# Two 64-row blocks to a tile, 75 chunks of edges for 78, and a load queue in the order of the stages

## What is computed

```python
# x [2048, 256], adj [2048, 2048], 8 heads of 32
scores = einsum('hnd,hmd->hnm', x * 32 ** -0.5, x2)
attn = softmax(where(adj > 0, scores, NEG))
x = layernorm(x + einsum('hnm,hmd->hnd', attn, v))
...
h = (x @ W_w.T + W_b)                       # second layer
e = leaky_relu(s_src[:, None] + s_dst[None, :], 0.2)
attn = softmax(where(adj == 0, NEG, e), axis=1)
out = layernorm(x + elu(attn @ h))
```

## Time and profile before

| | us |
|---|---|
| Median of 3 runs | 427.37 |
| The runs | 425.29, 427.37, 427.52 |
| The profiled execution's own time | 423.61 |
| Its span | 422.0 |
| VectorE busy | 298.7 (71%) |
| TensorE busy | 246.4 (58%) |
| GpSimd busy | 216.9 (51%) |
| ScalarE busy | 166.2 (39%) |

### The profile page before, as it was taken

The page is one execution under the profiler, slowest core; times in us unless marked ns, Lnnn a source line. Parts: engine busy times, 40 slices in busy tenths (PEclk is TensorE's granted clock), DMA queues, the critical chain, the costliest instruction groups (busy, mean ns, idle before and its releaser), DMA issues.

```text
span 422.0 us, 5435 instructions
## 1 busy us (share of the span) xinstructions
PE 246.4 (58%) x1394; PEld 175.0 (41%) x1394; DVE 298.7 (71%) x833; ACT 166.2 (39%) x473; POOL 216.9 (51%) x327
## 2 busy tenths in 40 slices
PE   0583454924677679778697988212571281396690
PEld 0463331613355457556464655111360160274460
DVE  2998498999999998999797858702350352657873
ACT  5414365432372464664425253000100251445635
POOL 7238556461775877726766311772777176164100
PEclk9995585795569686969798996655877575586886
DMA  8929618742776674412532400341444154142201
GB/s 294 375 52 372 262 68 283 237 117 99 259 251 211 209 306 122 121 39 66 147 121 57 123 29 29 92 112 35 112 112 108 38 131 106 55 115 77 67 25 56
DMA packets 24515, 57.93 MB, mean 137 GB/s; under 512 B 6592, under 2 KB 14912, under 8 KB 22432
## 3 DMA queue, kind: packets, MB, share of 16 engines
q0 software_dynamic: 10032, 31.77, 26.9%
q1 hardware_dynamic: 14448, 25.77, 17.1%
HBM read 53.20 MB, written 4.33 MB: 136 GB/s over the span
## 4 chain that ended last, share of the span: by engine, by line
PE 15%; DVE 14%; another core or an unknown queue 11%; issue 8%; POOL 6%; ACT 3%; DMA 1%; DVEq 0%; ACTq 0%; POOLq 0%
PE e_po L1445 8%; POOL e_ring L1071 5%; DVE e_weighted L1719 2%; PE e_pj L1468 2%; DVE e_y L1491 1%; DVE e_raw L1521 1%; DVE e_run L1690 1%; DVE e_run L1692 1%; DMA out<-e_prod 1%; DVE e_rden L1489 1%; DVE e_left L1719 1%; PE e_po L1426 1%; PE e_pq L1391 1%; DVE e_y L1742 1%
## 5 line engine op out<-in xcount | busy, mean ns | idle before, releaser
L1071 POOL DMA_INDIRECT e_ring<-in_kv,e_col_i x78 | 79.7, 1022 | 70.0 <-DVE e_col_i L1623 27.0
L1071 POOL DMA_INDIRECT e_ring<-table,e_col_i x78 | 74.4, 954 | 55.5 <-issue 23.0
L1445 PE MATMUL e_po<-e_weighted,e_sel_edges 128*128 128x264 f32 x158 | 52.0, 474 | 9.2 <-DVE e_weighted L1719 6.2
L1426 PE MATMUL e_po<-e_mean_row,e_diagonal 128*128 128x264 f32 x64 | 24.8, 479 | 37.5 <-DVE e_y L1491 22.9
L1445 PEld LDWEIGHTS e_po<-e_weighted,e_sel_edges 128*128 128x128 f32 x158 | 34.3, 232 | 19.5 <-DVE e_weighted L1719 9.8
L1164 ACT ACTIVATE e_search<-e_search 128x2048 bf16<-128x2048 int32 x16 | 30.5, 1908 | 26.4 <-DVE e_raw L1521 12.1
L1521 DVE MAX8 e_raw<-e_search 128x8 bf16<-128x512 bf16 (+2 forms) x56 | 38.7, 724 | 0.8
L1489 DVE RECIPROCAL e_rden<-e_po 128x8 f32<-128x8 f32 x32 | 6.5, 203 | 44.4 <-remote 20.2
L1391 PE MATMUL e_pq<-e_left,e_sel_rows 128*128 128x256 bf16 x156 | 33.3, 312 | 0.0
L1426 PEld LDWEIGHTS e_po<-e_mean_row,e_diagonal 128*128 128x128 f32 x64 | 12.6, 226 | 42.0 <-issue 40.5
L1445 PE MATMUL e_po<-e_left,e_search 128*128 128x264 f32 x84 | 27.9, 494 | 1.7 <-DVE e_left L1719 1.7
(11 more groups left out here) (221 smaller groups left out, 602.9 us busy)
## 6 DMA issues: line engine op xcount, KB each, us to landing
e_search<-in_adj SPq DMA_DIRECT2D x16, 1024.0 KB
table<-e_hx SPq DMA_DIRECT2D x16, 136.0 KB
e_ring<-in_kv SPq DMA_DIRECT2D x1, 2112.0 KB, 13.2
out<-e_prod SPq DMA_DIRECT2D x16, 128.0 KB
e_ring<-in_kv,e_col_i POOLq DMA_INDIRECT x78
e_ring<-table,e_col_i POOLq DMA_INDIRECT x78
e_xres<-in_x SPq DMA_DIRECT2D x2, 512.0 KB
e_xres<-in_x SPq DMA_DIRECT2D x3, 256.0 KB, 10.7
```

Of the source, the lines that this page charges most:

```text
L1071: nc.gpsimd.indirect_dma_start(out=rings[layer][:, q % RING[layer], :], out_offset=None, in_=kv if layer == 0 else table, in_offset=bass.I ...
L1426: nc.tensor.matmul(po[n % 2][:, 0:CV], diagonal[:, n % 3, :], mean_row[:], start=True, stop=False)
L1445: last = nc.tensor.matmul(po[n % 2][:, 0:CV], selection(layer, q, 1)[:, 0, :], weighted[plan.weighed_into(b)][:, j * CV:(j + 1) * CV], sta ...
```

## The change

- **Tiles.** A tile is no longer 128 consecutive rows but two blocks of 64 (`TILES`), one dense and one less dense from the fourth tile on. Every load of `adj` and x, every store to `table` and to the output becomes two transfers of 64 rows; the second halves of the first two tiles go out on ScalarE's queue.
- **Tables.** `CHUNKS` adds up to 75 (the big tile 13 instead of 16), `SEGS`, `GROUPS` and `KEEP` follow. The groups hold 7, 13, 12, 14, 15, 8 and 6 chunks instead of 8, 16, 12, 16, 9, 11 and 6, so the points at which GpSimd waits in layer 1 become q = 17, 30, 42, 56 and 71.
- **SyncE.** The w block goes out where the list puts the stage `w`, which now needs the load of the fifth tile; x of a later group goes out behind the loads of its own tiles.
- **Planner.** `FORESIGHT` goes from 0.1 to 0.2, and `w` is priced at 9.5 us on SyncE and 4 us more.

```diff
+BLOCK = 64
+TILES = ((0, 12), (1, 6), (2, 5), (3, 30), (4, 13), (7, 8), (9, 14), (10, 11), (15, 27), (16, 26), (17, 23), (18, 24), (19, 22), (20, 31), (21, 25), (28, 29))
-CHUNKS = (16, 8, 6, 5, 5, 4, 4, 4, 4, 4, 3, 3, 3, 3, 3, 3)
-SEGS = (16,) + (8,) * 2 + (4,) * 7 + (2,) * 6
+CHUNKS = (13, 8, 7, 5, 5, 5, 4, 4, 3, 3, 3, 3, 3, 3, 3, 3)
+SEGS = (16, 16, 8, 8) + (4,) * 8 + (2, 2, 4, 2)
-GROUPS = ((1,), (0,), (10, 11, 12, 13), (6, 7, 8, 9), (4, 5), (2, 3), (14, 15))
-KEEP = (24, 0, 16, 16, 24, 24, 16)
+GROUPS = ((2,), (0,), (8, 9, 10, 11), (6, 7, 12, 13), (3, 4, 5), (1,), (14, 15))
+KEEP = (24, 0, 16, 16, 24, 32, 16)
-FORESIGHT = 0.1
+FORESIGHT = 0.2
-    put("SP", 0.0, 0.0, ("w",), lag=34.0)
+    put("SP", 9.5, 0.5, ("w",), ("load", 4), lag=4.0)
-        put("SP", 0.0, 0.0, ("x", g), lag=(10.0, 12.0)[g] if g < 2 else 35.0)
+        put("SP", 1.2 * len(GROUPS[g]) if g > 1 else 0.0, g - 1.0 if g > 1 else 0.0, ("x", g), ("load", max(plan.k0[g] + len(GROUPS[g]) - 1, 5)) if g > 1 else None, lag=5.0 if g > 1 else (10.0, 12.0)[g])
...
-                sp.dma_start(adj_tile[:, k % 2, :], adj[t * P:(t + 1) * P, :]).then_inc(adj_loaded[k % 2], 16)
+                for i in range(1 if k < 2 else 2):
+                    sp.dma_start(adj_tile[half_of(i), k % 2, :], adj[rows_of(t, i), :]).then_inc(adj_loaded[k % 2], 16)
...
+                for j, t in enumerate(GROUPS[g]):
+                    for i in range(2):
+                        sp.dma_start(xres[half_of(i), plan.k0[g] + j, :], x[rows_of(t, i), :]).then_inc(x_loaded[g], 16)
...
             load_adj(2)
             load_adj(3)
-            sp.wait_ge(s("cleared"), 4)
-            sp.dma_start(w_sb[:], w_nat.rearrange("(k p) c -> p k c", p=P)).then_inc(s("w_loaded"), 16)
...
-            for g in range(2, NG):
-                load_x(g)
             for stage in stages:
                 if stage[0] == "load" and stage[1] >= 4:
                     load_adj(stage[1])
+                elif stage[0] == "w":
+                    sp.wait_ge(s("cleared"), 4)
+                    sp.dma_start(w_sb[:], w_nat.rearrange("(k p) c -> p k c", p=P)).then_inc(s("w_loaded"), 16)
...
+                elif stage[0] == "x" and stage[1] >= 2:
+                    load_x(stage[1])
...
+            for k in range(2):
+                act.dma_start(adj_tile[half_of(1), k, :], adj[rows_of(plan.order[k], 1), :]).then_inc(adj_loaded[k], 16)
             nc.scalar.preload_act_table_set("natural_log_exp_and_others")
```

More of the change, by code:

```diff
@@ L272, in listed @@
         g = plan.group_of_q(q)
-        return ("find_big", (q - plan.q0[g]) // 4 * 4 + 3) if g == BIG_GROUP else ("find", g)
+        return ("find_big", min((q - plan.q0[g]) // 4 * 4 + 3, plan.C[g] - 1)) if g == BIG_GROUP else ("find", g)
     def turned(layer, q):
@@ L296, in list_stages @@
             for p in range(parts_of[k]):
-                time = (3.35 if big else 0.8 if parts_of[k] == 4 else 1.3) + (1.25 if p == 0 else 0.0) + (2.5 if big else (0.9 if KEEP[g] == 16 else 1.35) if p == parts_of[k] - 1 else 0.0)
+                time = (3.35 if big else 0.8 if parts_of[k] == 4 else 1.3) + (1.25 if p == 0 else 0.0) + (2.5 if big else (0.45 * (KEEP[g] // TOP)) if p == parts_of[k] - 1 else 0.0)
                 kept_free = g and not big and p == parts_of[k] - 1
@@ L1010, in _ @@
                     sp.wait_ge(s("row_ready"), k + 1)
-                    sp.dma_start(table[t * P:(t + 1) * P, :], hx[:, k % 2, :]).then_inc(table_stored[k % 2], 16)
+                    for i in range(2):
+                        sp.dma_start(table[rows_of(t, i), :], hx[half_of(i), k % 2, :]).then_inc(table_stored[k % 2], 16)
                 elif stage[0] == "out":
@@ L1017, in _ @@
                     sp.wait_ge(s("emitted"), k + 1)
-                    sp.dma_start(out[t * P:(t + 1) * P, :], y_out[:, k % 2, :]).then_inc(out_stored[k % 2], 16)
+                    for i in range(2):
+                        sp.dma_start(out[rows_of(t, i), :], y_out[half_of(i), k % 2, :]).then_inc(out_stored[k % 2], 16)
         @block.gpsimd
@@ L1039, in _ @@
                 nc.gpsimd.memset(tile_base[:, k:k + 1], float(P * plan.c_first[t])).then_inc(s("const_ready"), 1)
-            nc.gpsimd.indirect_dma_start(out=xres[:, 0, :], out_offset=None, in_=x, in_offset=bass.IndirectOffsetOnAxis(ap=first_rows[:], axis=0)).then_inc(x_loaded[0], 16)
+            for i in range(2):
+                pool.dma_start(xres[half_of(i), 0, :], x[rows_of(plan.order[0], i), :]).then_inc(x_loaded[0], 16)
             pool.wait_ge(s("const_ready"), 3)
```

62 lines of the change are left out of this document (31 added, 31 removed).

## The result

| | before | with the change |
|---|---|---|
| Median, us | 427.12 (4 runs) | 442.32 (4 runs, 441.18 to 443.14) |
| Ratio to before, 95% interval | | 1.0415 (1.0373 to 1.0457) |
| Profiled execution, us | 423.61 | 442.53 |
| Its span, us | 422.0 | 440.9 |
| VectorE busy, us | 298.7 | 298.8 |

The change makes the kernel 4.2% slower. The forecast was 423.8 with a range up to 431.0: it had the sign wrong and the time lies outside the range.

A forecast was written before the change was run, and what follows sets the result against it. VectorE was taken to bound layer 0, gathers to pace layer 1. Start -1.5, VectorE's work -1.4, end of layer 0 -0.6, layer 1 -0.5, output +0.4 gave -3.6 us: 427.37 to 423.8, range 416.5 to 431.0.

The forecast's parts named there:

- The start: Up to the big tile's first round: VectorE idles 4.9 us instead of 6.9; -1.5 us, from -6 to +4.7.
- it is issued at about 20.0 instead of 32.99: On SyncE's queue at the start: the fifth tile's load leaves before the w block, once the third tile's sign is done.
- The rule against the change: Loads of adj into 64 partitions at half rate: third tile's sign 2.6 us later, time 426.4; chance 0.10.
- the block's length: SyncE's w block at the start: taken as 12.4 us, between bounds of 12.2 and 19.15.
- VectorE's work: Layer 0: draws +1.6, keep +1.1, fewer rounds -1.7, fewer chunks -0.8 for each of three lines; sum -1.4 us.
- In this stretch it counts in full: Layer 0: the -1.4 us of VectorE's work shortens the kernel by the whole amount.
- End of layer 0: Last tiles normed and projected: half of a projection half saved, -1.0, one more store issue, +0.4; -0.6 us (0 to -4).
- Layer 1: Gathers -3.75, first pause +1.3, tail +2.0: -0.5 us (-4 to +8); last output in two issues +0.4.
- The gathers set the pace: Layer 1: gathers of 0.94 us with 0.30 between, 1.25 us each, set its pace, interrupted by pauses.
- the tail of 29 chunks: Layer 1 from q = 71 on: 29 chunks to finish instead of 26, +2.0 us (0 to 3.8).
- The w block comes late: Rival at the start: block keeps 19.15 us, prefix sum at 45.0, VectorE waits; start +4.7, time 430.0; chance 0.12.
- the slow halves: Rival on loads of adj: halves at half rate, start +1.1, time 426.4; chance 0.10.

The follow-up runs named there:

- e10: The change, unedited, run again on a later chip beside the kernel before: 398.27 us, ratio 1.024 to the kernel before.
- e1: The kernel before with each adj load cut into two transfers of 64 neighbouring partitions, nothing else: 438.86 us, ratio 1.028 to the kernel before.
- e3: The changed kernel with halves interleaved in even and odd partitions instead of 0 to 63 and 64 to 127: 435.95 us, ratio 1.021 to the kernel before.
- e11: The same kernel as e3, on the chip of e10: 389.24 us, ratio 1.000 to the kernel before.
- e2: The kernel before with its own tiles, tables and whole-tile loads, and only SyncE's new order: 424.18 us, ratio 0.993 to the kernel before.
- e9: The kernel before, unedited, on the chip of e10: 389.61 us, ratio 0.999.
- e13: The change with sum_w behind the prefix sum, later turn_src behind the first turn, and stacked adj tiles in one transfer each: 622.71 us, ratio 1.470.
- e14: The change, unedited, repeated on the fourth further chip: 440.72 us, ratio 1.041 to the kernel before.

## Why the prediction was wrong

Between the -3.6 us forecast and the +18.9 us of the two traces lie 22.5 us: 10.3 of them in the start, 4.0 up to the last turn of layer 0, 2.0 to the end of layer 0 and 6.2 in layer 1.

**The start, -1.5 forecast, +8.8 measured (+7.7 in e10).** The step that failed is "it is issued at about 20.0 instead of 32.99". It took the third tile's sign to begin at 18.02 as before. The rule against the change was written down, its mechanism named and priced at 2.6 us, with a chance of 0.10. It held. The price was too small because it counted one tile: the halves ahead of it (the first two tiles', which I had taken to run at full rate side by side, and those of the third) add up, 8.0 us for the third tile's sign and 9.5 us for the end of the fifth tile's issues. The 2.6 us for a tile was about right in itself: the delay of the signs grows by 2.4, 2.4 and 3.2 us from tile to tile. e1 and e3 show that this cause alone makes +12 us on the old tables and takes 8.6 us (by the ratios) or 9.0 us (398.27 to 389.24 on one chip, e10 and e11) with it when it is taken out of the change. With whole tiles the failed step holds: in e2 the fifth tile's load is out at 20.34.

**The w block.** That `sum_w` would hold up the prefix sum was forecast with 2.9 to 9.6 us of idle time; it was 12.20 with slow halves and 8.95 without (e3). The term that failed is the block's length: 12.4 taken, 14.6 measured in e3 (21.18 to 35.8) and 15.6 in the change. The slow issues of `b_row` remained (3.95 and 5.17 us), with one tile alone ahead of them. What it costs in time, once the halves are scattered, is some 2 us at most, since VectorE does other work meanwhile. (The lower bound of 12.2 in the prediction is 12.5 by its own terms, which changes nothing.)

**VectorE's work, -1.4 forecast.** To the last turn of layer 0 its busy time is 209.97 us in e9 and 209.94 in e10: 0. In the first traces it is 209.05 and 210.36: +1.3. Draws (+1.3 measured, +1.6 forecast), first rounds and score groups came as worked out. Missed were the second scan of the groups (L1692, now L1710), which had no term, and a slightly slower product (L1506, now L1524):

```profile
L1524 DVE TENSOR_TENSOR e_search<-e_search,e_code 128x2048 bf16<-128x2048 bf16 x16 | 20.1, 1257 | 9.2 <-ACT e_search L1182 9.1
...
L1710 DVE TENSOR_TENSOR_SCAN e_run<-e_pens,e_run 56x160 f32<-56x160 bf16 (+6 forms) x14 | 9.0, 646 | 0.5
```

These rows of the changed kernel's groups are 9.0 us for 7.3 before and 20.1 for 19.5. The stretch grew by 2.6 to 3.2 us all the same: in e10 VectorE waits 4.4 us for a group's "back" where it waited 1.3 in e9. "In this stretch it counts in full" was right of work and forgot waits.

**End of layer 0, -0.6 forecast.** -0.6 in e10; +1.4 in the first trace.

**Layer 1, -0.5 and +0.4 forecast.** +6.1 on chips with late signals, -3.8 on those without. The forecast read one chip's trace as the kernel's nature, but that is not what made it wrong, for the change was first measured on the same kind of chip. "The gathers set the pace" is the sentence that was wrong for that kind: the gathers fewer bring 3.8 us, and pauses that end by TensorE's "back" cost 9.3 more. The pauses were forecast at 8.6, 8, 10 and 5 us and were 10.19, 9.57, 10.90 and 10.34, so over half of the error lies in the one ahead of q = 71, and why that one doubled no run tells. The reading of the chain left out the second long piece, of 11.91 us, ahead of the first pause. That q = 30 would not wait was right, and that the tail of 29 chunks costs 2.0 more was not: from the start of the last gather it took 31.1 us, for 30.7 before.

**The rivals.** "The w block comes late" was right that the prefix sum waits for a late block and VectorE for the prefix sum, and was given 430.0. It was wrong about why: the block did not keep its 19.15 us (it took 15.6), it began 8.6 us later. The late block and the slow halves were kept as two cases, and they are one, since the halves stand ahead of the block. Two rivals that share a queue happen together, and that case should have been priced. With the halves scattered the change still takes 1.021 on the first kind of chip; the traces put that on layer 0's waits (about 4 us from the first round to the last turn) and on layer 1's pauses, and no run takes the tables apart from the planner's order to say which of them brings the waits.

## What to carry to other kernels

A load into 64 neighbouring partitions ran at little more than half the rate of one into 64 scattered ones. So look at the partitions and not only at the bytes, and where a tile is dealt from two places scatter the halves (even and odd partitions) rather than stack them. When an order is changed for the sake of a late load, look at what the new first in the queue carries behind it: a wait inserted ahead of a short step on one engine (`sum_w` ahead of the prefix sum) holds every engine that needs the short step. And before a stretch is costed from one trace, ask whether its long pieces are "unknown" in the chain; what no instruction of the program explains may belong to the chip. Then a second chip tells more than a second run.

## What the runs showed of the hardware

- Transfers into 64 neighbouring partitions filled the DMA engines (share 0.98 to 1.03) at 210 to 232 GB/s; into 64 scattered ones, or all 128, they gave 378 to 403 while the engines were as full (share 1.03 to 1.06).
- Loads whose source has an outermost dimension of 2 ran at 58 GB/s together (e13, share 0.15).
- In the first traces and on two of the four later chips, TensorE's signals to ScalarE and VectorE were seen late, in the worst cases by 15 us and more (15.5 in the first trace of the change, 16.8 in e14, 18.1 in e1), while GpSimd issued indirect DMAs one behind another in layer 1; several came 3 to 4 us after it stopped, others while it went on. On the two others the same programs had none of this and ran layer 1 in 120 to 125 us instead of 158 to 165. In layer 0 of the first two traces and of e14 gathers came between other work, and such signals were at most some 2 us late. What differs in the chips is open.
